# Routed experts after attention: block rows loaded as quarters and transposed in 32x32 squares on VectorE

## What is computed

```python
x = x + xattn(_layernorm(x), ctx, ctx, Wq, Wk, Wv, Wo, padding_mask, attention_mask)   # 16 heads of 32
# the routed layer: the expert depends on the position only
idx = jnp.argmax(pe @ jnp.sign(tile_sigs).T, axis=-1)          # [S], 0 to 7
y_all = jnp.einsum('bsd,tod->bsto', _layernorm(x), W) + b
x = x + take_along_axis(y_all, idx)[:, :, 0]
```

## Time and profile before

| | |
|---|---|
| time, median of 3 runs | 953.64 us (953.4 to 953.99) |
| the profiled execution | 953.35 us, of which the span is 951.4 us |
| instructions | 16646 |
| TensorE matmul busy | 908.4 us (95%) |
| TensorE weight loads busy | 729.2 us (77%) |
| VectorE busy | 735.2 us (77%) |
| ScalarE busy | 383.9 us (40%) |
| GpSimd busy | 567.1 us (60%) |
| share of the chain that ended last, TensorE | 91% |
| line 1652 (expert products) in that chain | 21% |
| line 1632 (expert transposes) in that chain | 3% |
| DMA moved | 108.10 MB, 114 GB/s over the span |

### The profile page before, as it was taken

One profiled execution on the slowest core, in us unless ns is written; L12 is line 12 of the kernel. 1 busy time (PEld: TensorE's weight loads), 2 busy tenths in 40 slices (PEclk: granted clock), 3 DMA queues, 4 the chain that ended last, 5 costly groups with the idle time before them and its releaser, 6 DMA issues.

```text
span 951.4 us, 16646 instructions
## 1 busy us (share of the span) xinstructions
PE 908.4 (95%) x5696; PEld 729.2 (77%) x5697; DVE 735.2 (77%) x1097; ACT 383.9 (40%) x697; POOL 567.1 (60%) x763
## 2 busy tenths in 40 slices
PE   5899999999999999999999999999739999999997
PEld 4687887887888788788878878887627888888885
DVE  5988867777776877877787787779758777777775
ACT  5554444454544445454444545444451111111110
POOL 3855746465574646557464654743645777777773
PEclk9999999999999999999999999999878999999999
DMA  9613133131313314131331313113643544444551
GB/s 336 225 72 102 56 113 91 60 121 46 104 53 113 101 53 117 45 110 48 113 102 56 113 45 113 52 51 117 224 142 112 158 161 162 163 158 159 162 164 50
DMA packets 48876, 108.10 MB, mean 114 GB/s; under 512 B 10496, under 2 KB 15136, under 8 KB 46624
## 3 DMA queue, kind: packets, MB, share of 16 engines
q1 hardware_dynamic: 37216, 71.70, 23.7%
q0 software_dynamic: 11200, 35.21, 11.6%
q10 hardware_dynamic: 384, 0.21, 0.1%
HBM read 73.47 MB, written 35.19 MB: 114 GB/s over the span
## 4 chain that ended last, share of the span: by engine, by line
PE 91%; DVE 3%; POOL 2%; DMA 1%; issue 1%; ACT 0%; SPq 0%; DVEq 0%; POOLq 0%
PE pS L1358 27%; PE pA L1652 21%; PE pA L1358 20%; PE pS L1416 7%; PE pA L1439 7%; PE pT L1427 6%; PE pT L1632 3%; PE pS L1384 1%; DMA x_scratch<-y 1%; POOL xt_lo L982 1%; POOL wo_lo L1030 0%; DMA wk_raw<-in_wk 0%; DMA xg<-x_scratch,gather_rows 0%; PE pT L1463 0%; DVE early L1312 0%
## 5 line engine op out<-in xcount | busy, mean ns | idle before, releaser
L1652 PE MATMUL pA<-wf_hl,x_hi 128*128 x560 | 183.3, 409 | 1.9 <-DVE x_lo L1586 1.9
L1203 DVE TENSOR_TENSOR s<-pS,bias 128x1024 f32<-128x1024 f32 x64 | 78.0, 1219 | 100.3 <-PE pS L1416 100.3
L998 POOL COPY y<-y_mom 128x1 f32<-128x1 f32 x64 | 12.9, 202 | 238.5 <-DVE y_mom L1242 238.5
L1015 POOL TENSOR_TENSOR s<-s,row 128x1024 f32<-128x1024 f32 x64 | 122.0, 1906 | 11.5 <-DVE row L1223 11.5
L1119 ACT CAST ot_hi<-pA 128x512 fp32r<-128x512 f32 x64 | 37.6, 588 | 222.6 <-PE pA L1439 222.6
L1546 POOL DMA_INDIRECT out_dram<-y,scatter_rows x70 | 94.1, 1344 | 54.4 <-DVE y L1594 52.8
L1565 ACT CAST x_hi<-pT 128x512 fp32r<-128x512 f32 x70 | 41.1, 587 | 191.0 <-PE pT L1632 159.1
L1652 PEld LDWEIGHTS pA<-wf_hl,x_hi 128*128 128x128 f32 x560 | 101.1, 191 | 21.2 <-issue 2.3
L1358 PE MATMUL pA<-wo_hi,ot_hi 128*128 128x512 f32 x256 | 109.2, 426 | 4.5 <-DVE ot_lo L1227 4.5
L1652 PE MATMUL pA<-wf_hl,x_lo 128*128 x280 | 111.5, 398 | 0.0
L1358 PE MATMUL pS<-xt_hi,wq_hi 128*128 128x512 f32 x256 | 105.6, 413 | 3.9 <-DVE wq_lo L1262 2.3
(11 more groups left out here) (124 smaller groups left out, 1898.9 us busy)
## 6 DMA issues: line engine op xcount, KB each, us to landing
x_scratch<-y SPq DMA_DIRECT2D x64, 257.0 KB, 3.0
xt_raw<-in_x_t SPq DMA_DIRECT2D x16, 1024.0 KB, 6.2
x<-in_x SPq DMA_DIRECT2D x64, 256.0 KB, 2.6
wf_hl<-in_wf SPq DMA_DIRECT2D x8, 1024.0 KB, 8.8
ctx_raw<-in_ctx_t SPq DMA_DIRECT2D x32, 128.0 KB, 3.1
bias_all<-in_bf SPq DMA_DIRECT2D x1, 2048.0 KB, 10.8
mask_early<-in_mask SPq DMA_DIRECT2D x1, 1536.0 KB, 11.6
xg<-x_scratch,gather_rows POOLq DMA_INDIRECT x70
```

The source lines that it names most:

```text
L1015: pool.tensor_tensor(p, p, h.row[:, t % h.c, 3, :].unsqueeze(2).broadcast_to([P, H, BK]), ALU.mult)\
L1203: dve.tensor_tensor(h.s_sb[:, t % h.c, :].rearrange("p (h k) -> p h k", h=H), pS[:, 0, :].rearrange("p (h k) -> p h k", h=H), h.bias[:, t ...
L1652: mm = pe.matmul(pA[:, r % 2, :], a[:, c * P:(c + 1) * P], w, start=(c == 0 and m == 0), stop=(c == KC - 1 and m == 2))
```

## The change

Each row of y is now finished in attention in two forms. GpSimd adds the expert's bias (`add_bias`, 128x512, the bias gathered once per position into `bias_at`) and ScalarE normalises (`y_normalise`, 128x512, with -mean times rstd and rstd, which `y_rstd` now makes in three dependent steps). SyncE's `store_y` waits for both and writes the biased rows to `y_rows`, and the normalised rows as four quarters of 128 numbers (512 bytes) to `x_quarters`, laid out as 128 planes (quarter and sequence) by position.

In the expert stage a block's operand is loaded by four plain DMAs, one for each of its four positions (128 runs of 512 bytes each), at a position read into a register from a table in SBUF; SyncE issues two of them and ScalarE two. VectorE transposes the block in 32x32 squares (SBUF to SBUF); with the weight rows reordered on the host (`quarter_rows`), that is the operand that the product needs. TensorE's four transposes, the normalisation, the bias addition and the register load of VectorE's `add_bias` go from this stage. `high` and `low` now read SBUF where they read PSUM. GpSimd still gathers the residual rows (now biased) and scatters. VectorE's order for each j is `low(j+1)`, `transpose(j+2)`, `finish(j)`. Before its first `high`, ScalarE waits for all stores and issues the quarters of four blocks.

Besides: the low part of `wo` moves behind `normalise_p(0)` and is made in four pieces after VectorE's second `shifted`; the last store goes ahead of the load of expert 3; the load of all biases (2 MB) goes; VectorE has one small addition more in the prologue (`expert_at`), GpSimd two small gathers after tile 0 and one small copy after tile 6; `residual` waits for the two new results instead of the store.

```diff
-    x1 = nc.dram_tensor("x1_scratch", (B * S, DM + 2), F32, kind="Internal").ap()
+    y_rows = nc.dram_tensor("y_scratch", (B * S, DM), F32, kind="Internal").ap()
+    x_quarters = nc.dram_tensor("x_scratch", (KC * B, S, P), F32, kind="Internal").ap()
...
+        def store_rows(sp, rows, batch, half, ring):
+            sp.dma_start(y_rows[rows, :], y_biased[:, ring, :]).then_inc(y_stored[ring], 16)
+            dst = x_quarters.rearrange("(i b) s f -> b s i f", i=KC)
+            sp.dma_start(dst[batch, half * P:(half + 1) * P] if isinstance(batch, int) else
+                         dst[batch, half * P:(half + 1) * P].rearrange("a s i f -> (a s) i f"),
+                         y_normal[:, ring, :].rearrange("p (i f) -> p i f", i=KC)).then_inc(y_stored[ring], 16)
...
             def store_y(t):
-                sp.wait_ge(y_ready, t + 1)
-                sp.dma_start(x1[t * P:(t + 1) * P, :], h.y_sb[:, t % 2, :]).then_inc(y_stored[t % 2], 16)
+                sp.wait_ge(y_biased_ready, t + 1)
+                sp.wait_ge(y_normal_ready, t + 1)
+                store_rows(sp, slice(t * P, (t + 1) * P), t // 2, t % 2, t % 2)
...
                 store_y(h.tiles - 2)
-                sp.wait_ge(op_done, h.tiles)
+                store_y(h.tiles - 1)
                 load_expert_set(sp, LAST_FREE)
-                store_y(h.tiles - 1)
...
                 pool.wait_ge(y_mom_ready, t + 1)
-                pool.tensor_copy(y[:, DM:DM + 1], m[:, 0:1])
                 pool.tensor_scalar(m[:, 1:2], m[:, 1:2], EPS, None, ALU.add).then_inc(y_var_ready, 1)
...
+                pool.tensor_scalar(y[:, DM:DM + 1], m[:, 0:1], y[:, DM + 1:DM + 2], -1.0, ALU.mult, ALU.mult)\
+                    .then_inc(y_ready, 1)
+
+            def add_bias(t):
+                wait(pool, y_stored[t % 2], 32 * (t // 2))
+                pool.tensor_tensor(y_biased[:, t % 2, :], y_sb[:, t % 2, 0:DM], bias_at[:, t % 2, :], ALU.add)\
+                    .then_inc(y_biased_ready, 1)
...
-            pool.wait_ge(w_hi_ready["o"], 1)
-            pool.tensor_tensor(w_lo["o"][:].rearrange("p c n -> p (c n)"), wo_raw[:],
-                               w_hi["o"][:].rearrange("p c n -> p (c n)").bitcast(F32), ALU.subtract)\
-                .then_inc(w_lo_ready["o"], 1)
             xt_low(1)
             normalise_p(0)
+            pool.wait_ge(shifted, 2)
+            pool.wait_ge(w_hi_ready["o"], 1)
+            for c in range(KC):
+                ins = pool.tensor_tensor(w_lo["o"][:, c, :], wo_raw[:, c * DM:(c + 1) * DM],
+                                         w_hi["o"][:, c, :].bitcast(F32), ALU.subtract)
+            ins.then_inc(w_lo_ready["o"], 1)
...
+            def y_normalise(t):
+                y = y_sb[:, t % 2, :]
+                act.wait_ge(y_ready, t + 1)
+                wait(act, y_stored[t % 2], 32 * (t // 2))
+                act.activation(y_normal[:, t % 2, :], y[:, 0:DM], ACT.Identity, bias=y[:, DM:DM + 1],
+                               scale=y[:, DM + 1:DM + 2]).then_inc(y_normal_ready, 1)
...
-                for t in (4, 5, 6, 7, 3):
+                y_normalise(h.tiles - 2)
+                expert_high(act, 4)
+                y_normalise(h.tiles - 1)
+                for t in (5, 6, 7, 3):
                     expert_high(act, t)
...
             def residual(t):
                 dve.wait_ge(op_done, t + 1)
-                wait(dve, y_stored[t % 2], 16 * (t // 2))
...
+                wait(dve, y_normal_ready, t - 1)
+                wait(dve, y_biased_ready, t - 1)
...
+        def gather_quarters(eng, j, quarters):
+
+            r = j % R
+            wait(eng, x2t_ready, j + 1 - R)
+            _, at = nc.values_load_multi_w_load_instructions(
+                position_of[0:1, j, quarters.start:quarters.stop], engines=[eng.engine], min_val=0, max_val=S - 1,
+                skip_runtime_bounds_check_because="a position comes from a one-hot product with the numbers 0 to 255")
+            for s, n in zip(at, quarters):
+                eng.dma_start(xq[:, r, n * P:(n + 1) * P],
+                              x_quarters[:, bass.ds(s, 1), :].rearrange("p a f -> p (a f)")).then_inc(quartered[r], 16)
+
+        SYNC_QUARTERS, SCALAR_QUARTERS = range(0, 2), range(2, PB)
+
+        def experts_sync(sp):
+            sp.wait_ge(positions_known, 1)
+            for j in range(NR):
+                gather_quarters(sp, j, SYNC_QUARTERS)
...
+            act.wait_ge(positions_known, 1)
+            for b in range(2):
+                act.wait_ge(y_stored[b], 32 * SHORT.tiles // 2)
+            for j in range(R - 2):
+                gather_quarters(act, j, SCALAR_QUARTERS)
             for j in range(NR):
                 high(j)
+                if j + R - 2 < NR:
+                    gather_quarters(act, j + R - 2, SCALAR_QUARTERS)
...
-            def add_bias(j):
-                e = dve.value_load(expert_of[0:1, j:j + 1], min_val=0, max_val=NE - 1)
-                dve.tensor_tensor(xb[:, j % 2, :], xg[:, j % R, 0:DM],
-                                  bias_all[:, bass.ds(e, 1), :].rearrange("p a n -> p (a n)"), ALU.add)\
-                    .then_inc(xb_ready, 1)
-
-            def normalise(j):
+            def transpose(j):
                 r = j % R
-                wait(dve, x2t_done, j - 1)
-                dve.wait_ge(gathered[r], 16 * (j // R) + 16)
-                dve.tensor_scalar(xn2[:, j % 2, :], xg[:, r, 0:DM], xg[:, r, DM:DM + 1], xg[:, r, DM + 1:DM + 2],
-                                  ALU.subtract, ALU.mult).then_inc(xn2_ready, 1)
+                dve.wait_ge(quartered[r], 16 * PB * (j // R) + 16 * PB)
+                wait(dve, x2_lo_ready, j - 1)
+                dve.transpose(x2t[:, j % 2, :].rearrange("p (c g b) -> p c g b", c=KC, g=PB),
+                              xq[:, r, :].rearrange("p (g c a) -> p c g a", g=PB, c=KC)).then_inc(x2t_ready, 1)
...
-            def transpose(k, n):
-                j, r, turn = at(k, n)
-                pe.wait_ge(xn2_ready, j + 1)
-                wait(pe, x2_lo_ready, j - 1)
-                for c in range(KC):
-                    mm = pe.transpose(pT[:, r % 2, c * P:(c + 1) * P], xn2[:, r % 2, c * P:(c + 1) * P], ident[:])
-                mm.then_inc(x2t_done, 1)
...
+                product(k, n, expert(k, n))
...
+def quarter_rows():
+
+    c, i, n = np.meshgrid(np.arange(KC), np.arange(KC), np.arange(DH), indexing="ij")
+    return (P * i + DH * c + n).reshape(-1)
...
-        "wf": a["L0_ffn_W"].transpose(0, 2, 1),
+        "wf": a["L0_ffn_W"].transpose(0, 2, 1)[:, quarter_rows(), :],
```

More of the change, by code:

```diff
@@ L282, in kernel_program @@
         wf_loaded = [sem(f"wf_loaded_{t}") for t in range(NE)]
-        wf_hi_ready = [sem(f"wf_hi_ready_{t}") for t in range(NE)]
+        wf_hi_ready = sem("wf_hi_ready")
+        HIGH_ORDER = (0, 1, 2, 4, 5, 6, 7, 3)
         wf_lo_pool = sem("wf_lo_pool")
@@ L621, in full_scalar @@
                 group(i)
-            for t in FIRST_FREE + LATER_FREE + LAST_FREE:
+            for t in HIGH_ORDER:
                 expert_high(act, t)
@@ L1050, in tiles @@
                         xt_low(g + 2)
+                    if t == 0:
+                        gather_bias(pool)
+                    if t == 2:
+                        pool.wait_ge(bias_loaded, 32)
+                    if t >= 2:
+                        add_bias(t - 2)
+                    if t == 6:
+                        order_positions(pool)
                     if t == h.tiles - 2:
@@ L1057, in tiles @@
                 y_rstd(h.tiles - 2)
+                add_bias(h.tiles - 2)
                 y_rstd(h.tiles - 1)
+                add_bias(h.tiles - 1)
             return tiles
@@ L1315, in short_vector @@
             moments(1)
+            done(dve.tensor_scalar(expert_at[:], r1[:, 1, :], float(2 * NE), None, ALU.add))
             done(dve.tensor_tensor(expert_f[:], c_block[0:1, :].unsqueeze(2).broadcast_to([1, NR, NE - 1]),
@@ L1522, in kernel_program @@
         y2 = sb("y2", [P, 3, DM])
-        xb_ready = sem("xb_ready")
         gathered = [sem(f"gathered_{r}") for r in range(R)]
-        xn2_ready = sem("xn2_ready")
-        x2t_done = sem("x2t_done")
+        quartered = [sem(f"quartered_{r}") for r in range(R)]
+        x2t_ready = sem("x2t_ready")
         x2_hi_ready = sem("x2_hi_ready")
@@ L1601, in experts_vector @@
             expert_low(dve, 5)
-            normalise(0)
-            normalise(1)
+            transpose(0)
+            transpose(1)
             expert_low(dve, 6)
             low(0)
-            add_bias(0)
             for j in range(NR):
@@ L1610, in experts_vector @@
                 if j + 2 < NR:
-                    normalise(j + 2)
+                    transpose(j + 2)
                 if j == 0:
@@ L1656, in body @@
             def body(k, n):
-                first = isinstance(k, int) and R * k + n == 0
-                if first:
-                    transpose(k, n + 1)
-                if is_block(k, n):
```

(12 more changed lines are left out.)

123 lines of the change are left out of this document (74 added, 49 removed).

## The result

On the machine of the first comparison the changed kernel took 958.25 us (median of 5, 957.57 to 958.8) and the kernel before 953.99 (5 runs, 953.4 to 954.71): a ratio of 1.0051, 95% interval 1.0036 to 1.0066. It is slower by half a per cent, where 926.7 was forecast. Later runs put the same unchanged file beside the kernel before on two chips: 955.67 on one (ratio 1.0028, 1.0018 to 1.0039) and **925.84 on the other (ratio 0.9710, 0.9688 to 0.9732)**. The kernel before took 953.2 to 954.3 in all six comparisons: this first one and one on each of the five chips of the experiments. I call chips on which the changed kernel reaches 925 the first kind, and those on which its signals are late, as in the first result, the second.

What follows compares the result with a forecast made beforehand. TensorE was taken as the bound, so work leaving it shortens the kernel: -31.0 (expert blocks) + 0 (attention) - 3.0 (prologue) + 7.4 (start of experts) = -26.6, from 953.35 to 926.7 us; range 919 to 948, about 0.8.

Steps and rivals of the forecast that it cites:

- Expert blocks, -31.0: Expert stage: without transposes a block takes 2.79 us in place of 3.24, if every other engine keeps up; -31.0 us.
- VectorE: Expert blocks: low, finish and the new transposition (taken 0.69 us) sum to 2.06 us, at most 2.74, under 2.79.
- ScalarE and SyncE: Expert blocks: two DMA issues each per block at register positions, taken as 1.7 us, so high is in time.
- the rival of 3.9 us a block: Expert blocks: two register loads and two slow issues ahead of each high bound the pace; 1003 us, chance 0.12 with slow DMA.
- GpSimd and the DMA engines: Expert blocks: GpSimd 2.6 to 3.05 us, taken as keeping 2.79; DMA 2.3 to 2.6 us of 2.79.
- another engine sets the pace: Rival, expert blocks: GpSimd at 3.04 us or DMA at 2.9 to 3.1 sets the pace; 943 us, chance 0.22.
- Attention, 0: Attention tiles: GpSimd's addition of 1.27 us and ScalarE's pass of about 0.6 fit the slack; 0 us, up to +3.
- Prologue, -3.0: Prologue: with xt_lo early, TensorE's 1.57 us wait and slower matmuls go; -3.0 us, bounds -4.5 to 0.
- Start of the experts, +7.4: From attention to experts: first product at 723.6 in place of 716.15; +7.4 us, bounds +2 to +14.
- Steps 2 and 3: Start of experts: expert 3's load lands at 712.0, high part 713.9; then ScalarE's quarters and VectorE's work, until 723.6.
- Step 1: Start of experts: add_bias(63) starts with VectorE's low part of expert 2; done at 701.3 or 703.6, taken 703.0.
- TensorE's time only turns into waiting at 3.24 a block: Rival, expert blocks: transpose, high and low follow each other too slowly, TensorE waits for low; 958 us, chance 0.03.

Runs made afterwards that it cites:

- n1: The changed kernel, unchanged, as control on the fourth chip, of the first kind: 925.84 us, the kernel before 953.20.
- c1: The changed kernel, unchanged, run again on the third chip, with late signals: 955.67 us, the kernel before 953.28.
- o1: Changed kernel, from the seventh block one fixed-address DMA of 512 packets in place of four, on the fifth chip: 952.46 us, the kernel before 953.79.
- c2: Changed kernel with three buffers each for x2_hi, x2_lo and the products' PSUM banks, on the third chip: 954.97 us, the kernel before 953.28.
- e7: Changed kernel with TensorE's register load of the next expert number moved into the middle of a product, second chip: 955.84 us, the kernel before 953.92.
- e8: Changed kernel where TensorE waits for all eight low parts, a constant, instead of a register's number, second chip: 960.91 us, the kernel before 953.92.
- c3: Changed kernel where TensorE loads the expert number once and all blocks use its matrix, third chip: 949.79 us, the kernel before 953.28.

## Why the prediction was right or wrong

The sum was -31.0 + 0 - 3.0 + 7.4. Step by step, with the spans of n1 (924.4 us) and of the first result (956.2) against 951.4:

- **Expert blocks, -31.0.** From the first product to the end of the last: before 228.3 us (716.15 to 944.49), n1 192.9 (724.83 to 917.70), so **-35.5**. The product is twelve times 0.227 us (2.72 from 755.28 to 758.00 above), not 0.232. The 0.232 was read rightly: with the transposes between them, the matmuls of a block start 0.229 to 0.237 us apart from the third to the last; in n1 they start 0.226 to 0.228 apart. That the pitch would stay was taken without a reason; why it changes isn't shown. The first result has 226.4 us (723.20 to 949.56), so **-2.0**. This is the step that failed: "if every other engine keeps up with 2.79 us". Each engine does keep up by its own durations. What didn't keep up was a signal between them, which the sum had at nothing. The prediction gave the round trip from a product through `finish` to `low` a slack of 1.4 us; a signal that is 2.5 us late uses it up. 21 late signals at 1.6 us are 33.6 us, and the two traces differ by 35.5 - 2.0 = 33.5. No row of before shows a late signal.
- **VectorE.** Transposition 705 ns (taken 0.69 us), `low` 693, `finish` 678. Right.
- **ScalarE and SyncE.** In the first result a register load takes 0.48 to 0.50 us and an issue 0.33 to 0.36 (medians); in n1 ScalarE's register load takes 0.85, and `high` is in time even so. Right; the rival of 3.9 us a block didn't occur.
- **GpSimd and the DMA engines.** Gather 0.98, scatter 1.12 to 1.13; the DMA share is 0.93 at full pace, within 0.8 to 0.95. Right, and the rival "another engine sets the pace" isn't seen on the first kind.
- **Attention, 0.** `y_biased` takes 1.27 us (the mean of 55 is 1265 ns) and `y_normal` 0.82; the tiles keep their distance to before within 0.01 us from tile 4 to tile 60. Right.
- **Prologue, -3.0.** The wait for `xt_lo` is gone (below, TensorE at 41.33), and the first tile is 4.25 us earlier (44.95 against 49.20). By tile 3 only 1.5 us of it is left, in c1 2.1, in n1 0.6. The time line of the first result, TensorE and GpSimd:

```profile
41.33 0.66 PE L1455 MATMUL pS<-ident,k 128*128 128x128 f32 x4 [1.16 <-ACT vd L1154]
46.98 5.05 POOL L1079 TENSOR_TENSOR wo_lo<-wo_raw,wo_hi 128x512 fp32r<-128x512 f32 x4 [2.08 <-DVE s L1281]
55.22 0.98 PE L1498 MATMUL pT<-ident,s 128*128 128x128 f32 x7 [1.37 <-POOL s L1060]
```

  `normalise_p(1)` now has `wo_lo` ahead of it, as I had named, and TensorE waits 1.37 us for it. I took the near end of a bound whose other end I had a reason for.
- **Start of the experts, +7.4.** Forecast 723.6 for the first product, without the prologue's 3 us; it came at 723.20, in n1 at 724.83. Against its own last tile (`residual(63)` at 697.24 before, 696.13 and 696.99 after) that is 1.1 + 7.05 = 8.2 us later in the first result and 0.25 + 8.7 = 8.9 in n1. Steps 2 and 3 have the order that was put: load of expert 3, its high part, then ScalarE's quarters, which land 4.0 us after their issue. That 723.20 is so near to 723.6 is partly luck: in the first result the load is issued 1.3 us sooner than was put and takes 7.6 us in place of 8.2, but ScalarE's first quarter leaves only at 714.27, 2.3 us after the high part ends at 712.01, for which the sum had nothing. Step 1 is the time of `add_bias(63)`, first result and then n1:

```profile
700.42 1.09 POOL L1045 TENSOR_TENSOR y_biased<-y,bias_at 128x512 f32<-128x512 f32 x1
700.50 7.84 DVE L310 TENSOR_TENSOR wf_hl<-wf_hl 128x2048 fp32r<-128x2048 f32 x3 [2.66 <-POOL y L1040]
```

```profile
701.33 7.59 DVE L310 TENSOR_TENSOR wf_hl<-wf_hl 128x2048 fp32r<-128x2048 f32 x3 [2.64 <-POOL y L1040]
701.64 2.93 POOL L1045 TENSOR_TENSOR y_biased<-y,bias_at 128x512 f32<-128x512 f32 x1 [0.34 <-DMA x_scratch<-y_normal]
```

  GpSimd started 0.08 us ahead of VectorE and took 1.09, while VectorE's first low part took 3.16 in place of 2.29; or it started 0.31 us behind, held up by the store before, and took 2.93: some 2 us until VectorE's first low part is done (2.3 us), then 1 us of its own. Both ends occur, one in each run, and the value between them that I took in neither. All traces of the changed kernel and its variants fit: GpSimd takes 1.09 us in the 15 in which it starts first, 2.93 to 3.22 in the three in which it starts 0.02 to 0.31 us behind, and 1.95 in o1, where it starts 1.29 behind. That agrees with 'SBUF — State Buffer' in the Trainium skill, 'Who interferes with whom', that the ports which both share are an exclusive lock, for which a VectorE instruction with two SBUF inputs contends with a GpSimd instruction that reads SBUF.
- **Sum.** n1: -35.5 + 8.7 = -26.8, near the 924.4 - 951.4 = -27.0 of the spans and the -26.6 of the forecast, because the blocks gave 4.5 us more and the start and prologue together took 4.3 more: two errors that cancel, and luck as far as the number goes. The first result: 7.05 - 2.0 = +5.0 (spans +4.8).
- **Rivals.** The one that gave 958 ("TensorE's time only turns into waiting at 3.24 a block") has the number of the first result and its pace, at a chance of 0.03. Its mechanism was another one: `transpose`, `high` and `low` are fast enough, as n1 shows. The range of 919 to 948 had no case for a delay between engines that isn't in anyone's duration.

**What stays open** is why `f_done` is late on some chips, and why in every third or fourth block. Shown on such chips: it isn't the number of operand or PSUM buffers (c2), the place of TensorE's register load (e7), its wait on a register's value (e8), or the count of the quarters' DMAs alone (o1). Without TensorE's register loads (c3) the signals are still late, though less often, and the time is 949.79 in place of 955.67. Not tried on such a chip: without quarters' bytes, without gathers, without scatters. Two rivals no run here can tell apart: each chip served one batch, so a lasting property of the chip and a state of it at that time look alike; and every timed execution here has its span and granted clock recorded, so that the recording itself takes part isn't excluded.

## What to carry to other kernels

A kernel whose bound engine never waits hides what its signals cost; when a change removes that engine's surplus, the round trip from product to `finish` and `high` and back becomes the thing to price, with some slack for a signal that is 2.5 us late. Put the unchanged kernel into every batch of experiments: without it, eight clean-looking runs on two chips supported a cure that the ninth and tenth refuted. And a pitch that was measured beside the work which a change removes can be another without it: 0.233 us with the transposes between the products, 0.227 without.

## What the runs showed of the hardware

- Chips differ in a way that one kernel shows (925.84 against 955.67 us for the same file) and another doesn't (953.20 against 953.28). The DMA engines themselves aren't slower on the second kind: their busy shares of 0.80 (c1) and 0.93 (n1) from 740 to 900 us, for 50 and 59 blocks, are 2.56 and 2.52 us a block. The window of c1:

```profile
740.00:900.00 160.00, 140.43 (x600) 110.86 (x599) 97.76 (x150) 30.49 (x50) 104.54 (x100) 1.00 0.80 242
```

- The traces mark the two kinds. In n1 1,462 semaphore updates are recorded from 800 to 840 us; in the first result there are 477, though the blocks are only a sixth fewer, and those around a late signal come in bursts about 0.7 us apart. So GpSimd's gathers have a time to landing in the issues of n1 (first line, its last number) and none in those of the first result (second line):

```profile
yg<-y_scratch,gather_rows POOLq DMA_INDIRECT x70, 5.1
```

```profile
yg<-y_scratch,gather_rows POOLq DMA_INDIRECT x70
```

  Of the 1,120 updates that 70 gathers make (16 each), n1 records 1,114 and the first result 520. The trace of before has 981 and no time to landing either, with every `f_done` in time, so a missing landing time alone doesn't foretell late signals. The counts fit a common delay of semaphore updates, of which the late `f_done` is the part that hurts; that is an argument, not a result.
- VectorE's transposition in 32x32 squares of 128x512 float32 takes 0.705 us, about as much as a subtraction or an addition of that size (`low` 0.693, `finish` 0.678).
